# Loading a stage's weights before the division, and dummy matmuls in two waits of TensorE, in a fused attention and gated feed-forward layer

## The reference

```python
q, k, v = _proj_heads(x, w_q, 16), _proj_heads(x, w_k, 16), _proj_heads(x, w_v, 16)
scores = einsum('bhqd,bhkd->bhqk', q, k) / sqrt(64) + mask      # causal
out = einsum('bhqk,bhkd->bhqd', softmax(scores), v)             # heads joined again
x = _layernorm(x + einsum('bsv,mv->bsm', out, o_proj_weight))

xr = mu_r * x + (1.0 - mu_r) * x_prev                           # x_prev: x one token earlier
xk = mu_k * x + (1.0 - mu_k) * x_prev
r = sigmoid(xr @ W_r)
x = _layernorm(x + r * (square(relu(xk @ W_k)) @ W_v))
```

## Time and profile before

| | us |
|---|---|
| time, median of 2 runs | 3299.95 (3294.46 and 3305.44) |
| profiled execution, its time | 3297.8 |
| profiled execution, span of the slowest core (core 5) | 3296.8 |
| spans of the other cores | 3271.6 to 3288.9 |
| TensorE busy (matmuls) | 1983.8, 60% of the span |
| VectorE busy | 1349.4, 41% |
| ScalarE busy | 1010.9, 31% |
| mean granted TensorE clock, core 5 | 0.735 of full |

### The profile page before, as it was taken

How to read it: one execution, slowest core, us unless ns; L and a number is a source line. 1 busy time by engine, 2 the same in 40 slices (tenths; PEclk the granted TensorE clock), 3 DMA queues, 4 the chain that set the end, 5 groups by cost and what they waited for, 6 DMA issues and landing times.

```text
span 3296.8 us, 29095 instructions; the slowest of 8 cores (3271.6 to 3296.8 us)
## 1 busy us (share of the span) xinstructions
PE 1983.8 (60%) x7360; PEld 834.9 (25%) x7360; DVE 1349.4 (41%) x2858; ACT 1010.9 (31%) x1385; POOL 40.8 (1%) x81
## 2 busy tenths in 40 slices
PE   3346786666666584563653887666666665636535
PEld 3333342222222212221221433222222211212212
DVE  2233333444444454344342333444444463433433
ACT  0000003555555402323322001555555511233233
POOL 1110000000000000000000000000000000000000
PEclk8557998777777756776866998777677755858767
DMA  5554100000000011101104000000000003011010
GB/s 167 166 169 150 47 18 7 5 4 5 5 4 5 4 60 68 51 1 51 41 11 140 26 27 20 4 4 4 4 4 4 4 4 128 1 51 51 0 51 26
DMA packets 35453, 131.27 MB, mean 40 GB/s; under 512 B 8800, under 2 KB 13024, under 8 KB 32480
## 3 DMA queue, kind: packets, MB, share of 16 engines
q0 software_dynamic: 11088, 73.41, 7.1%
q1 hardware_dynamic: 24208, 56.00, 5.3%
HBM read 93.47 MB, written 31.46 MB: 38 GB/s over the span
## 4 chain that ended last, share of the span: by engine, by line
PE 45%; DVE 25%; issue 10%; DMA 9%; ACT 9%; DVEq 1%; ACTq 0%; SPq 0%; POOL 0%; POOLq 0%
PE PV L342 9%; PE qk L249 7%; PE S L418 7%; PE kp L739 4%; PE v L786 3%; PE vv L268 3%; DMA x<-x 3%; ACT P L451 3%; ACT P L443 2%; DVE dg L378 2%; DVE dg L375 2%; PE pp L127 2%; PE bc L494 2%; DMA xs<-x 2%; PE tf L690 2%
## 5 line engine op out<-in xcount | busy, mean ns | idle before, releaser
L443 ACT ACTIVATE P<-S,eb 128x1024 bf16<-128x1024 f32 (+7 forms) x512 | 379.9, 742 | 1344.3 <-PE S L418 1329.4
L342 PE MATMUL PV<-P,V 128*65 128x512 bf16 (+3 forms) x1280 | 431.8, 445 | 335.1 <-DVE P L462 328.5
L418 PE MATMUL S<-qh,K 128*128 128x512 bf16 (+3 forms) x1280 | 473.0, 449 | 120.5 <-ACT P L443 49.7
L451 ACT ACTIVATE P<-S,eb 128x512 bf16<-128x512 f32 (+1 forms) x384 | 317.4, 827 | 13.6 <-PE S L418 8.9
L457 DVE TENSOR_TENSOR P<-P,tr 128x128 bf16<-128x128 bf16 x512 | 115.4, 225 | 424.5 <-ACT P L443 382.7
L342 PEld LDWEIGHTS PV<-P,V 128*65 128x65 bf16 x1280 | 149.1, 133 | 541.1 <-issue 492.1
L249 PE MATMUL qk<-xf,sl 128*128 128x512 bf16 x1024 | 238.6, 398 | 15.7 <-DVE xf L231 15.7
L418 PEld LDWEIGHTS S<-qh,K 128*128 128x128 bf16 x1280 | 130.2, 112 | 433.7 <-issue 410.0
L638 PE MATMUL op<-fs,O 128*128 128x512 bf16 x512 | 141.2, 445 | 155.2 <-DVE x L650 102.5
L739 PE MATMUL kp<-xk,fs 128*128 128x512 bf16 x512 | 132.7, 421 | 157.7 <-DVE xk L718 157.5
L127 PE MATMUL pp<-idf_s,wst 128*128 128x128 f32 x448 | 105.3, 417 | 154.9 <-DMA wst<-wkf 21.9
(11 more groups left out here) (84 smaller groups left out, 1941.7 us busy)
## 6 DMA issues: line engine op xcount, KB each, us to landing
xs<-x SPq DMA_DIRECT2D x32, 512.0 KB, 4.3
fs<-wscr POOLq DMA_DIRECT2D x8, 2048.0 KB, 22.8
x<-x SPq DMA_DIRECT2D x32, 512.0 KB, 5.0
y<-x SPq DMA_DIRECT2D x32, 512.0 KB, 3.0
wscr<-wasm POOLq DMA_DIRECT2D x7, 2048.0 KB, 9.5
sl<-wscr POOLq DMA_DIRECT2D x6, 2048.0 KB, 24.1
wst<-wq POOLq DMA_DIRECT2D x8, 512.0 KB, 4.1
wst<-wk POOLq DMA_DIRECT2D x8, 512.0 KB, 4.5
```

Of the source, the lines that this page charges most:

```text
L342: mi = TE.matmul(out=PV_ps[0:65, a:b], lhsT=Vp[:, 1040 * jj + 65 * h:1040 * jj + 65 * h + 65], rhs=P[jj % 2][0:128, a - 128 * jj:b - 128 * ...
L418: mi = TE.matmul(out=S_half[half][:, o:o + b - a], lhsT=K[:, T * qtile + 128 * j: T * qtile + 128 * j + 128], rhs=qh[h % 2][:, a:b], start ...
L443: ai = SE.activation(out=P[j % 2][:, 0:szA], in_=S_half[0][:, off0:off0 + szA], func=AF.Exp, bias=ebias[:], scale=0.125)
L451: ai = SE.activation(out=P[j % 2][:, szA:szA + szB], in_=S_half[1][:, 0:szB], func=AF.Exp, bias=ebias[:], scale=0.125)
```

## The change

Two things are changed, in both sequences.

The counters' values are noted at the end of the attention stage, ahead of the division (`pre_div`), and POOL waits for these instead of `at_end` before it loads the four weight matrices. The waits of the SP queue stay as they are.

A function `te_bridge(n)` puts n matmuls of 128 x 128 by 128 x 512 (bfloat16, on the first weight matrix) into TensorE's stream, without a wait and without a count; their result goes into a PSUM tile `dum_ps` of its own, which nothing reads. 32 of them stand in each span between the o-projection of the fourth tile and the first transpose, and 24 between the last transpose and kp. That is 56 for each of eight spans, 448 in all.

```diff
--- before.py
+++ after.py
@@ -467,6 +467,8 @@
                                 emit_pv(h, 15)
                                 emit_chunk_epilogue(h, 3, qtile, poff)
 
+                        pre_div = dict(st=st.v, sv=sv.v, ss=ss.v)
+
                         VE.wait_ge(dst_s[0].h, dst_s[0].v)
                         VE.wait_ge(dst_s[1].h, dst_s[1].v)
                         VE.wait_ge(ost_s[0].h, ost_s[0].v)
@@ -546,10 +548,18 @@
                     lnNB = ff.enter_context(nc.sbuf_tensor(f"lB{s}", [128, 4], F32))
                     murs = ff.enter_context(nc.sbuf_tensor(f"mr{s}", [128, 8], F32))
                     muks = ff.enter_context(nc.sbuf_tensor(f"mu{s}", [128, 8], F32))
-
-                    GP.wait_ge(st.h, at_end["st"])
-                    GP.wait_ge(sv.h, at_end["sv"])
-                    GP.wait_ge(ss.h, at_end["ss"])
+                    dum_ps = ff.enter_context(
+                        nc.psum_tensor(f"du{s}", [128, 512], F32))
+
+                    def te_bridge(n):
+                        for _ in range(n):
+                            TE.matmul(out=dum_ps[:], lhsT=fslots[0][:, 0:128],
+                                      rhs=fslots[0][:, 0:512],
+                                      start=True, stop=True)
+
+                    GP.wait_ge(st.h, pre_div["st"])
+                    GP.wait_ge(sv.h, pre_div["sv"])
+                    GP.wait_ge(ss.h, pre_div["ss"])
                     fsl = [wsl_s[i].dma(GP.dma_start(out=fslots[i][:],
                                                      in_=wscr[3 + i]))
                            for i in range(4)]
@@ -664,6 +674,7 @@
                                                    func=AF.Identity,
                                                    accum_out=lnS[:, u:u + 1])
                                 sq1st[i] = ss.inc(sq)
+                            te_bridge(32)
                             VE.wait_ge(ss.h, sq1st[4 * sp + 3])
                             ln1r = ln_batch()
                             for u in range(4):
@@ -721,6 +732,7 @@
                                     in1=x1f_r[:, ch, 0:512],
                                     op0=ALU.mult, op1=ALU.add)
                                 mixdone[(sp, ch)] = sv.inc(mk)
+                            te_bridge(24)
                         with ExitStack() as ps2:
                             k_ps = [ps2.enter_context(
                                 nc.psum_tensor(f"kp{s}{sp}{i}", [128, 512], F32))
```

## The result

| | before | after |
|---|---|---|
| median, us (all runs made of each) | 3297.72 (16 runs) | 3264.83 (17 runs) |
| ratio after / before, 95% interval | | 0.990 (0.987 to 0.993) |
| span of the profiled execution, slowest core | 3296.8 | 3262.5 |
| spans of all cores | 3271.6 to 3296.8 | 3247.0 to 3262.5 |

The change saves 33 us (1.0%); 37 us and a time of 3263 were forecast. In some executions of any of these kernels, the one before too, the cores of one die get a lower clock and the time is longer: the medians hold them, the ratios leave out the clearly slow ones.

A forecast was written before the change was run, and what follows sets the result against it. A chain of short stages waiting for each other, the first span's early part bound by one DMA burst. Early loads -36.9, bridges 0 and 0: -37 us, 3260.9 against the profiled execution, 3263 on the runs' median; range 3248 to 3278.

The forecast's parts named there:

- The weight loads: Four loads issued ahead of the division: last lands 32.5 us after issue, 38 us ahead of T, the division's end.
- the small row: Last 2 KB `dn<-dg` load before the division, meeting the first weight load: cost 0 to 1.7 us per sequence, taken as 0.
- The new schedule: First span after the division's end T: last residual sum at T + 18.1 instead of T + 36.7; gain 36.9 us over both sequences.
- The bridges: Dummy matmuls before transposes (32) and kp (24): no cost, gain 0 each, since idle time outlasts the clock's hold.
- the upper bounds of the prediction: Most the bridges could gain: 30 us for all transposes, 7 for each span's first group, 17 for kp.
- The rival of a cold o-projection: First span behind the division: clock stays low through 64 matmuls, 27.5 us; gain only 15.5 us, 3284; chance 0.07.
- The rival of a lowered clock: Denser TensorE work lowers the granted clock in rp, v and kp: +73 us, 3336, at c = 0.83; chance 0.03.
- the level of 13/16: Current limiter's clock once a third core of a die runs dense matmuls: +84 us, 3347; no row showed it.
- The rival that the bridges work: Bridges hold the clock through transposes and kp: -84 us in all, 3216; chance 0.04 (first group alone 3256, 0.08).

The follow-up runs named there:

- other_three_early: Changed kernel without bridges, only the three later weight matrices loaded ahead of the division, the first behind it: 3284.66 us, 0.995 of the kernel before.
- first_matrix_early: Changed kernel without bridges, only the first weight matrix (o-projection) loaded ahead of the division, the other three behind it: 3302.6 us, 0.998 of the kernel before.
- bridge1_58: Changed kernel with 58 instead of 32 dummy matmuls in the first bridge, before the transposes: 3262.28 us, 0.986 of the kernel before.
- bridge2_76: Changed kernel with 76 instead of 24 dummy matmuls in the second bridge, before kp: 3248.92 us, 0.981 of the kernel before.
- bridges_late: Changed kernel with bridges of 28 and 24 matmuls that wait for the last sum of squares and the fourth mix: 3251.23 us, 0.986 of the kernel before.
- bridges_late_between: The late-starting bridges of 28 and 24 matmuls, plus 7 matmuls between the groups of transposes: 3223.41 us, 0.976 of the kernel before.

## Why the prediction was right, step by step

**The weight loads.** Predicted hidden whole behind the division: the last lands 26.3 us after issue, at about 1174, 44 us ahead of T. POOL issued 0.6 us after the end that it waits for, as assumed, and the small row landed in 1.6 us against 1.7: cost 0, as taken.

**The new schedule.** Predicted T + 7.2 for the first sum and T + 18.1 for the last; measured T + 8.1 and T + 18.5 on the slowest core, where the o-projection started at T + 0.6 and not T + 0.1, and 7.3 and 17.7 as means. The order of the waits is as laid out: the sums wait for the matmuls, and the last x load, issued at 1229.9 and landing 5.0 us later at the latest, is there before its sum at 1235.50. The one thing that wasn't typical is what it was compared with. Core 5, the slowest core and the only one that was read, had T + 36.7 and 36.4; the mean over cores was T + 35.2. The stage gained 35.8 us over both sequences where 36.9 was forecast, and other_three_early and first_matrix_early show that both waits had to go for it. That the time came within 2 us of 3263 is in part luck: the forecast took 37 us off a median of two runs, 3299.95, and the change took 33 us off one of 16 runs, 3297.72.

**The bridges.** Predicted 0 and 0: 0.2 us and 1.6 us of 1112 by the two experiments that have one half each. The reason given, that the clock doesn't outlast the rest, is shown by bridge1_58, bridge2_76 and bridges_late: bridges of the same kind work as soon as the rest is short, and gain what the upper bounds of the prediction said (17 us for kp, measured 16.5; 7 us for the first group, measured 7.5; 30 + 17 for all, measured 40.8). This step was close: a hold of 5.3 us in the span shown, a rest of 6.2; the clock fell inside the rest in all 64 spans.

**The rival of a cold o-projection** is out: 62 matmuls took 16.43 us and not 27.5. **The rival of a lowered clock** didn't come true: rp stands at 379 ns on all eight cores in the profiled execution of every kernel with bridges. But the level of 13/16 that it named exists here, against the two levels of the rows: 0.81 in first_matrix_early, which has no bridges, with rp at 418 ns as a mean on core 4 in sequence 1. It also stood for 3 to 5 us of sequence 0's first o-projection, ahead of any bridge, on cores 4 to 7 of bridges_late and cores 4 and 5 of bridges_late_between. What brings it on no run here varies, so that stays open. **The rival that the bridges work** described a real mechanism at the wrong size; its price was right and its condition was not met.

## What to carry to other kernels

A load whose buffer is free earlier than its wait says belongs at the earlier point, above all when it shares the DMA engines with small loads that are wanted at once: one burst can make two waits, and here taking away either alone gained little over a third of what both gained (5.9 and 6.9 of 17.5 us).

Dummy work that is to keep TensorE's clock up must end close to the real work: here rests of up to 2.1 us kept the clock up to kp, those of 2.3 to 2.9 us often didn't, and those of 6.1 us or more never did. So size or time it from the far end of the wait, and look at the duration of the first real instructions behind it (here 272 or 417 ns). Half of the first wait and a third of the second, filled from the near end, were worth nothing. 28 matmuls in the right place did more than 32 in the wrong one, and the pauses of 2.2 us between the short groups of transposes needed their own filling.

## What was not expected

The float32 transposes gain more from the high clock than their number suggests: a group of eight goes from 1.94 to 1.06 us, and it stands four times in a serial chain of TensorE and ScalarE in each span. But eight transposes in every 3.2 us didn't keep the clock up by themselves (bridge1_58: high for the first one or two groups, then low), while with seven dummy matmuls in each pause all 256 ran high. The rest after which the clock fell varied in one and the same kernel, behind the bridges of the change, between 2.0 and 5.4 us.
